# Two of five stores moved from the SP queue to a queue of GpSimd's own, in a gated residual kernel

## What is computed

```python
h = silu(cond @ W1.T + b1)
gate = sigmoid(h @ W2.T + b2)[:, None, :]     # (128, 1, 512)
# v = x; Haar levels: details (e-o)/sqrt(2), a = (e+o)/sqrt(2); all times gate; inverse
return x + (v + a)                            # x: (128, 128, 512) f32
```

## Time and profile before

| | |
|---|---|
| time, median of 3 runs | 166.62 us (166.60 to 166.67) |
| profiled execution | 166.82 us, span from first to last instruction 165.1 us |
| busy time of DVE | 80.0 us, 48% of the span |
| busy time of PE, POOL, ACT | 22.7, 2.6, 2.5 us |
| moved by DMA | 69.47 MB, mean 421 GB/s over the span |
| chain that ended last | DMA 50%, DVE 19%, PE 12% |

### The profile page before, as it was taken

How to read it: one execution, slowest core, us unless ns; L and a number is a source line. 1 busy time by engine, 2 the same in 40 slices (tenths; PEclk the granted TensorE clock), 3 DMA queues, 4 the chain that set the end, 5 groups by cost and what they waited for, 6 DMA issues and landing times.

```text
span 165.1 us, 219 instructions
## 1 busy us (share of the span) xinstructions
PE 22.7 (14%) x68; PEld 12.2 (7%) x68; DVE 80.0 (48%) x20; ACT 2.5 (2%) x3; POOL 2.6 (2%) x10
## 2 busy tenths in 40 slices
PE   0099969800000000000000000000000000000000
PEld 0093722300000000000000000000000000000000
DVE  0052380499999999999970000000004999700000
ACT  3000100100000000000000000000000000000000
POOL 6000000000000000000000000000000000000000
PEclk9999987995555555555555555555555555555555
DMA  5999969969998997989997996999899799799995
GB/s 151 474 456 508 476 286 508 508 286 476 508 397 365 508 508 254 508 349 413 508 429 334 508 508 302 461 508 413 349 508 445 334 492 508 318 445 405 445 421 254
DMA packets 1732, 69.47 MB, mean 421 GB/s; under 512 B 194, under 2 KB 194, under 8 KB 324
## 3 DMA queue, kind: packets, MB, share of 16 engines
q1 hardware_dynamic: 1008, 43.25, 61.4%
q10 hardware_dynamic: 724, 26.22, 36.9%
HBM read 35.92 MB, written 33.55 MB: 421 GB/s over the span
## 4 chain that ended last, share of the span: by engine, by line
DMA 50%; DVE 19%; PE 12%; DVEq 5%; ACT 1%; issue 0%
DMA ring<-in_x 23%; DMA out<-ring 22%; DVE ring L242 10%; DVE ring L247 5%; DVEq L30 5%; DMA ring<-in_L_cond_W 5%; PE gate_sum L173 3%; PE turned L181 2%; PE hidden_sum L151 2%; PE turned L135 2%; DVE ring L229 2%; PE hidden_sum L146 1%; PE turned_cond L140 1%; DVE factor L237 0%; DVE ring L222 0%; ACT ring L193 0%
## 5 line engine op out<-in xcount | busy, mean ns | idle before, releaser
L242 DVE TENSOR_TENSOR ring<-ring,factor 128x16384 f32<-128x16384 f32 x3 | 51.5, 17220 | 0.0
L247 DVE TENSOR_TENSOR ring<-ring,factor 128x8192 f32<-128x8192 f32 x2 | 17.3, 8688 | 40.5 <-DMA ring<-in_x 40.5
L216 DVE COPY ring<-turned 128x512 f32<-128x512 f32 x4 | 2.8, 692 | 10.0 <-PE turned L135 10.0
L237 DVE TENSOR_SCALAR factor<-turned 128x512 f32<-128x512 f32 x4 | 2.8, 691 | 6.9 <-PE turned L181 6.9
L173 PE MATMUL gate_sum<-ring 128*128 128x512 f32 x8 | 5.4, 833 | 1.3 <-DVE ring L227 1.3
L135 PE MATMUL turned<-identity,ring 128*128 128x128 f32 x16 | 3.6, 423 | 8.4 <-DMA ring<-in_L_cond_W 8.4
L229 DVE COPY ring<-turned 128x512 f32<-128x512 f32 x4 | 3.9, 1056 | 0.0
L135 PEld LDWEIGHTS turned<-identity,ring 128*128 128x128 f32 x16 | 3.3, 227 | 8.4 <-issue 8.4
L181 PE MATMUL turned<-ring 128*128 128x512 f32 x8 | 3.7, 601 | 0.8 <-ACT ring L193 0.8
L151 PE MATMUL hidden_sum<-ring 128*128 128x512 f32 x8 | 3.7, 605 | 0.0
L222 DVE TENSOR_TENSOR ring<-hidden_sum,ring 128x512 f32<-128x512 f32 x1 | 0.7, 692 | 5.6 <-ACT ring L190 5.6
(11 more groups left out here) (17 smaller groups left out, 6.6 us busy)
## 6 DMA issues: line engine op xcount, KB each, us to landing
out<-ring ACTq DMA_DIRECT2D x2, 4096.0 KB, 20.8
ring<-in_L_cond_W ACTq DMA_DIRECT2D x1, 1024.0 KB, 7.7
ring<-in_L_cond_W SPq DMA_DIRECT2D x1, 1024.0 KB, 7.5
ring<-in_cond SPq DMA_DIRECT2D x1, 256.0 KB, 7.7
ring<-in_x SPq DMA_DIRECT2D x3, 34.6
b_row<-in_L_cond_b ACTq DMA_DIRECT2D x2, 2.0 KB
out<-ring SPq DMA_DIRECT2D x2, 45.6
ring<-in_x ACTq DMA_DIRECT2D x1, 38.6
```

The source lines that it names most:

```text
L216: dve.tensor_copy(w1_t[:, c, :], turned[c][:, :]).then_inc(w1_t_set, 1)
L242: dve.tensor_tensor(ring[:, c, :, :], ring[:, c, :, :], steps_of(c, STEPS), ALU.mult).then_inc(chunk_scaled, 1)
L247: dve.tensor_tensor(ring[:, 0, piece(h), :], ring[:, 0, piece(h), :], steps_of(CHUNKS - 1, PIECE), ALU.mult).then_inc(chunk_scaled, 1)
```

## The change

SP no longer issues stores 0 and 1. GpSimd does, at the end of its program, with the same waits, the same access patterns and the same semaphores; its DMAs go through a queue of its own. Nothing else is changed.

```diff
             sp.wait_ge(gate_spread, GROUPS)
             sp.dma_start(ring[:, SCRATCH, :, :], chunk(x_parts, SCRATCH)).then_inc(chunk_loaded[SCRATCH], DMA_DONE)
 
-
-            for c in range(SLOTS - 1):
-                sp.wait_ge(chunk_scaled, c + 1)
-                sp.dma_start(chunk(out_parts, c), ring[:, c, :, :]).then_inc(chunk_stored[c], DMA_DONE)
-
         @block.gpsimd
...
             pool.affine_select(out=spread, in_=spread, compare_op=ALU.is_ge, fill=0.0, base=GROUPS - 1,
                                pattern=[[-P, GROUPS], [-1, P]], channel_multiplier=GROUPS).then_inc(spread_set, 1)
+
+
+            for c in range(SLOTS - 1):
+                pool.wait_ge(chunk_scaled, c + 1)
+                pool.dma_start(chunk(out_parts, c), ring[:, c, :, :]).then_inc(chunk_stored[c], DMA_DONE)
```

## The result

The changed kernel takes 167.36 us (median of 20 runs, 166.60 to 168.09), the kernel before 166.76 on the same chip (20 runs, 166.52 to 167.25). The ratio is 1.0026, with a 95% interval of 1.0013 to 1.0038: slower by a quarter of a per cent. The forecast was no change, 166.6. The times are not shifted as a whole. Of the 20 runs, 7 lie between 166.60 and 166.83, where the kernel before has its median, and 13 between 167.12 and 168.09; of the kernel before 5 of 20 lie over 167.0. So something happens in two of three executions that costs 0.4 to 1.3 us, and in the others the change costs nothing. The profiled execution (167.61 us, span 165.9) is one of the 13.

A forecast was written before the change was run, and what follows sets the result against it. The prediction took the sixteen DMA engines, at share 1.00 from 13 to 160 us, as the bound. All terms summed to 0 on the profiled 166.82 us, so the median stayed at 166.6 us; range 166.2 to 168.4.

The forecast's parts named there:

- the 52.6 of the prediction: The time in us from which store 0 and load 2 were to alternate packets, store 0 being issued at 51.23.
- What the prediction priced at zero on GpSimd, SP, DVE and ACT: Waits and issues moved from SP to GpSimd, DVE's later chunk 2, store 2's later issue on ACT: each 0.
- a cover of 16.6: Load 2 alone would keep the DMA engines busy 16.6 us past store 0's issue, so its issue-to-first-byte time costs 0.
- Store 1 beside load 3: Store 1 and load 3 share the engines from GpSimd's and ACT's queues instead of SP's and ACT's: 0.
- Store 0 moves out from behind load 2: Store 0 alternates with load 2 and lands at 86.6, not 87.3: gain 0 to 0.7 us, none reaching the end.
- The new queue moves bytes less well: Rival: small packets or heavier set-up and close of GpSimd's queue, 167.0 to 168.3, likeliest near 167.5; chance 0.19.
- GpSimd held up by DVE: Rival: store 0's descriptors wait for DVE's second multiplication, 168.1, or until DVE is idle, 185.2; chances 0.09 and 0.03.

The follow-up runs named there:

- experiment 4: Kernel before, but GpSimd issues store 1, only when chunk 2 is scaled, and store 0 stays in SP's queue: 170.63 us, ratio 1.024.
- experiment 7: Changed kernel, but GpSimd waits for load 2 to land before store 0, so store 0 no longer runs beside load 2: 170.65 us, ratio 1.0255.
- 9: Changed kernel, but GpSimd clears the identity matrix 32 times before store 0, so store 0 meets less of load 2: ratio 1.0012.
- experiment 1: Kernel before, but ACT issues stores 0 and 1 and SP load 3; three sets: 1.0036 (profile quick), 1.0011, 1.0024 (profile slow).
- experiment 8: Kernel before, but GpSimd issues everything after load 2, two sets: 1.0030, 1.0049; in a third kernel GpSimd issues only store 0, ACT the rest: 1.0036.

## Why the prediction was wrong

Set out by order, with what the runs gave (experiments 4, 7 and 9 are left out):

| chunk transfers | ratio to before | over 167.0 |
|---|---|---|
| store 0 behind load 2 (before, all sets) | 1 | 18 of 142 |
| the same, other orders (late DVE; one queue; store 1 by GpSimd) | 1.0004, 1.0012, 0.9999 | 5 of 35 |
| store 0 beside load 2, later ones in ACT's queue | 1.0004, 1.0021 | 6 of 23 |
| store 0 beside load 2 and store 1 beside load 3, hardware queues | 1.0036, 1.0011, 1.0024 | 22 of 36 |
| the same with GpSimd (the change) | 1.0026, 1.0019 | 19 of 32 |
| the same, store 0 by GpSimd and store 1 by SP (experiment 2) | 1.0025 | 8 of 12 |
| store 0 beside load 2, in GpSimd's queue, others in GpSimd's or ACT's | 1.0030, 1.0049, 1.0036 | 21 of 29 |

*The order of events was right.* Load 2 was put at 81.7 and landed at 79.6; store 0 at 86.6, landed at 86.9; store 2 near 99, issued at 96.9. The engines do take turns by equal packets, though later than the 52.6 of the prediction: store 0's first packet ran at 57.1, 4.5 us after its issue, and 5.7 us after it in ACT's queue (experiment 1, first profile). What the prediction priced at zero on GpSimd, SP, DVE and ACT shows no cost in the trace; GpSimd's time from issue to first byte with the DMA engines idle, bounded by 0.7 to 1.2 us, is 1.3 (experiment 7), under a cover of 16.6.

*The step that failed* is the term "Store 1 beside load 3 [...] Equal packets from two queues either way: 0". It rested on the DMA share of 1.00 and the rates of the earlier trace rows, and both are means over sixteen engines. A share of 1.00 says that the engines have packets under way all the time; it does not say that each packet takes 2.42 us. Where loads and stores meet, a packet may take 2.9 to 3.7 us on one or three engines, with the share still at 1.00. Every transfer is done when its slowest engine is done, and with no slack a late engine stays late. What was put at 0 measured +0.8 us in the profile (load 3's landing) and 0.6 in the difference of the medians. The term "Store 0 moves out from behind load 2" has the same fault: it counts packets for all engines alike and gives a gain of 0 to 0.7, while the engine that ends last had 0.3 us of its delay from there. That the new order costs the time, and not GpSimd's queue alone, is shown by experiment 1. The long round at the first meeting stood in the trace of the kernel before (3.26 us a packet); the prediction did not read packets round by round.

*The rivals.* "The new queue moves bytes less well" named a time near 167.5, and the time came out near there, but not for its reason: packet size and price are unchanged, and hardware queues in the same order lose as much. So it is luck that 167.36 lies inside the range of 166.2 to 168.4, which was stretched for other reasons. "GpSimd held up by DVE" did not show: its issues took 0.68 and 0.53 us while DVE multiplied, and its first packet ran at 57.1 us, as did ACT's in experiment 1. The Trainium skill (page "SBUF — State Buffer", section "SBUF: two separate sides") warns of such a stall while DVE runs a 2-port perf-mode op. The limit that the Trainium skill gives on the same page, section "Who interferes with whom", as an inference, is that `tensor_tensor` takes only the read interface of the shared ports; the trace agrees with it.

*A slip that changed nothing:* of the two times to landing of L204 in the earlier trace rows, the longer belongs to the last piece. It lands at 143.3 + 21.3 = 164.6 and not at 163.5; the stretches view shows nothing after 163.4 because it books a packet at its start.

*What stays open.* Why a meeting hits some engines and not others. Whether the second stretch is worse when store 0 ran beside load 2 before it, or the first stretch alone costs most of the time: the table points to the former and does not settle it. The packets' records have a pattern here. In the changed kernel's profile, the slow one of experiment 1 and the second set's of experiment 8, eight engines are hit hard at a later meeting (by 0.5 to 1.3 us), and seven of these had lost 0.2 to 0.5 us at 57 us, in the first stretch; they are the last of the sixteen to begin that later round, in one case the last but one. A late engine thus tends to be hit again, but not always: in the quick profile of experiment 1 the last to begin were not. Open, too, is whether GpSimd's queue adds to it: with two stretches there is no sign of it (means 167.23 with it, 167.17 without), with one there is (167.37 and 167.30 against 166.98).

## What to carry to other kernels

When the DMA engines are busy throughout, moving a transfer to another queue moves no work, and issuing it earlier gains nothing; what can still change is how evenly the sixteen engines get through, and the end follows the slowest. Here the order with two stretches of loads and stores in turns lost 0.1 to 0.4%, while taking the last of them away gained nothing over one. So do not add such a stretch for nothing, and look at one round of packets at a time, since a mean share of 1.00 hides an engine that is a microsecond late. And look at the spread of the times before explaining a quarter of a per cent: here it was a loss of about a microsecond in some executions, and nothing in the others.

## What the runs showed of the hardware

Right before the first packets of the first store, the load's packets take longer on all sixteen engines, by 0.8 us in the mean before and 0.6 after (3.26 and 2.99 us instead of 2.42); in experiment 7, where that store began after a pause, they do not. Later meetings cost between nothing and 1.3 us per engine, and up to 1.7 us after the pause of experiment 7; they differ from one execution to the next of the same kernel. A store issued by GpSimd has packets of the same size and duration as one from SP or ACT, and needs 1.3 us from issue to first byte when the DMA engines are idle. One kernel whose TensorE program was unchanged (experiment 4) ran the eight matmuls of a group at 1152 ns instead of 605 in the profiled execution, while its trace gives the granted clock as 1.00 throughout, the higher of the two levels, 2.4 GHz, so that the record and the matmuls do not agree there.
